# Loading the first four pairs' expert weights inside the recurrence instead of among the sorted rows

## The chip, the cores and the metric

The kernel runs on one core of one Trainium2 chip. The metric is the device time of one execution in microseconds, as the median of the runs shown. Without another unit, all times here are microseconds, and places in the trace are counted from the start of the profiled span.

## The reference, cut to what matters

Two layers are computed on 1024 tokens of 256 channels. Each layer normalises x, computes an attention part `s` and a mixture of experts `g` from the same normalised tokens, and adds `s * silu(g)` to x. The change lies in the second layer. Its attention part is a gated linear recurrence over the tokens with an output product and a small MLP behind it:

```python
def step(S, inp):
    qt, kt, vt, gt = inp
    S = S * jnp.exp(gt)[..., None] + kt[..., None] * vt[..., None, :]
    ot = jnp.einsum('bhk,bhkd->bhd', qt, S)
    return (S, ot)
...
logits = flat @ router_w
_, topk_idx = jax.lax.top_k(logits + router_bias, K)     # K = 4 of E = 64 experts
...
g = jax.nn.silu(jnp.einsum('nd,edf->nef', flat, wg))     # F = 64 hidden channels an expert
u = jnp.einsum('nd,edf->nef', flat, wu)
routed = jnp.einsum('ne,nef,efd->nd', comb, g * u, wd)
```

`wg` and `wu` hold 256 x 64 numbers for each expert, `wd` 64 x 256, all float32.

## The kernel before, in words

The second layer is `gated_linear_attention`. It is a row of blocks; all engines meet at the end of each. Two of them are touched.

**The recurrence's block.** It projects the tokens, routes them, and runs the recurrence in 16 steps (`STEPS = 2 * GK`), each with a scan on DVE over all tokens (L2159). PE sums a step's heads (`gathered_step`, L1941) and counts `o_step` up. Until step 7 PE also computes the output gates (`gates`) from the weights `wg`. Meanwhile POOL scatters each token's row to its four places in a DRAM tensor, `sorted_tokens`, in the order of the experts (L1807). A token has four experts, so there are 4096 sorted rows. The router also makes a table of windows: 64 main windows, one for each expert, of 128 sorted rows, and 32 extra ones for experts with more rows. SP writes the table to DRAM and reads it back (`store_table`, `table_loaded`). Last in SP's program come the loads of the first eight blocks of 256 sorted rows, `load_rows` (L1798), when all rows are scattered; there are eight row buffers.

**The pairs' block.** First comes the row stage. PE transposes the recurrence's output (`turn_state`, L2391, eight tiles) and the sixteen blocks of sorted rows (`turn_rows`, L2401); ACT copies the even blocks from PSUM to `xTs` (L2319), DVE the odd ones (L2214). When all are there, the 48 pairs of windows follow (`Blocks1`). They are worked in the order main, main, extra. For each pair q:

- SP loads its gate and up weights into one of four raw buffers and its down weights into one of eight down buffers (`Blocks1.load`, L1599 to L1609): three DMAs of 128 KB for a main pair; for an extra pair two reads of the table into registers and six DMAs of 64 KB. From q = 4 on it waits until pair q-4 is laid out, from q = 8 on until the down product of pair q-8 is done.
- POOL lays the weights out (`lay`, L1618), four pairs ahead at most.
- PE multiplies gate and up (`gate_up`, L1639, eight matmuls), two pairs ahead of down; ACT applies silu, DVE multiplies (`hidden`, L1693), PE multiplies down (L1651), ACT copies the result and stores it to DRAM.

Beside the pairs run the parts of the shared experts, of the output product and of the normalisation, each tied to a number of a pair (`side`). A pair with an even number from 0 to 14 carries one half of the shared experts' gate and up (L1494 to L1496, twelve matmuls).

The order of SP's queue in the pairs' block is written out by hand: row blocks 8 to 15, each when the block eight before it is turned, and behind every second of them the weights of one pair, so of the pairs 0 to 3; then the pairs from 4 on.

SBUF places are given by hand too. `shelf(start, end)` hands out places between two offsets in KB. The masks of the recurrence (`spread`, `gather_h`) lie at 165 to 171, the first products' weights (`wq`, `wk`, `wv`, `wg` and others) at 171 to 182, the router's work buffers at 182 to 194. The pairs' buffers lie from 165 on, over all of these, and so can be filled only when the recurrence has ended.

Of the kernel before, what the change touches and what calls it, by code (L numbers as in the profile page):

```python
# [13 lines left out]
P = 128  # L14
T = 1024
NT = T // P
D = 256
DC = D // P
# [22 lines left out]
E1, F1, K1 = 64, 64, 4  # L41
# [11 lines left out]
class Chain:  # L53
# [3 lines left out]
    def __init__(self, engine, done):  # L57
        self.engine, self.done, self.count = engine, done, 0
# [1483 lines left out]
class Blocks1:  # L1542
# [4 lines left out]
    PAIRS = WINDOWS // 2  # L1547
    EXTRA = OVER // 2
    RAW, LAID, DOWN, HIDDEN, GROUP = 4, 4, 8, 3, 4

    def __init__(self, nc, env, w, router, xTs, weights, results):
        self.psum, self.table, self.xTs = env["psum"], router.table, xTs
        self.gu_src, self.dn_src = [w["L1_ffn_" + k] for k in ("wg", "wu")], w["L1_ffn_wd"]
        self.y_dram = nc.dram_tensor("block_outputs", [WINDOWS * P, D], F32, kind="Internal").ap()
        sem = env["sem"]

        self.nc, self.at = nc, {}
        self.order = [pair for i in range(self.EXTRA) for pair in (self.EXTRA + 2 * i, self.EXTRA + 2 * i + 1, i)]
        self.raw_loaded = [sem(f"e1_ld{b}") for b in range(self.RAW)]
        self.dn_loaded = [sem(f"e1_dl{b}") for b in range(self.DOWN)]  # L1560
        self.main_stored = [sem(f"e1_ms{b}") for b in range(2)]
        self.extra_stored = [sem(f"e1_xs{b}") for b in range(2)]
        self.laid, self.gu_ready, self.silu_ready, self.h_ready, self.y_ready, self.y_done = (
            sem("e1_" + s) for s in ("la", "gu", "si", "h", "y", "yd"))
        self.raw = [weights(f"e1_raw{b}", [P, 2, 2, DC, F1]) for b in range(self.RAW)]
        self.gu = [weights(f"e1_gu{b}", [P, 2, DC, 2, F1]) for b in range(self.LAID)]
        self.dn = [weights(f"e1_dn{b}", [P, D]) for b in range(self.DOWN)]
        self.sg, self.hf = ([weights(f"e1_{n}{b}", [P, cols]) for b in range(self.HIDDEN)] for n, cols in (("sg", 2 * P), ("hf", P)))
        self.main_y = [results(f"e1_ym{b}", [P, 4, D]) for b in range(2)]
        self.extra_y = [results(f"e1_yx{b}", [P, 2, D]) for b in range(2)]  # L1570
# [127 lines left out]
def gated_linear_attention(nc, env, w, out):  # L1698
# [8 lines left out]
    def at(kb, name, shape, dt=F32):  # L1707

        return nc.alloc_sbuf_tensor_at("g_" + name, shape, dt, offset=int(kb * 1024))

    def shelf(start, end):

        place = [int(start * 1024)]

        def put(name, shape, dt=F32):
            here, size = place[0], int(np.prod(shape[1:])) * SIZE[dt]
            place[0] = here + -(-size // 32) * 32
            assert place[0] <= end * 1024, (name, place[0])
            return nc.alloc_sbuf_tensor_at("g_" + name, shape, dt, offset=here)
        return put  # L1720

    keep = shelf(194, 208)
    router = Router1(nc, env, w, keep)
# [27 lines left out]
    xTs = at(25, "xTs", [P, DC, SLOTS1 + P])  # L1751
    ROW_BUFFERS = 8
# [1 line left out]
    ogT, equal, wo = at(66, "ogT", [P, DC, T]), at(74, "equal", [P, NT, E1]), at(76, "wo", [P, DC, D])  # L1754
    shared.work_buffers(shelf(141, 157), shelf(58, 66))
    x2r, x2T_h, x2T_l = at(97, "x2r", [P, NT, D]), at(81, "x2T_h", [P, DC, T], F16), at(85, "x2T_l", [P, DC, T], F16)
    blocks = Blocks1(nc, env, w, router, xTs, shelf(165, 194), shelf(208, 224))
    mlp = at(58, "mlp", [P, 2, SplitWeights.SHARED - SplitWeights.W1], F16)
    yg = at(25, "yg", [P, NT, K1, D])
    late_at = shelf(141, 175)  # L1760
# [8 lines left out]
    def square(act, source, which, n):  # L1769
# [18 lines left out]
    v_spread, kv_ready, st_ready, qs_ready, o_step, oT_done, z_read, e_made, ln_made, dec_made = (  # L1788
        sem("g2_" + s) for s in ("v", "kv", "st", "qs", "o", "oT", "zr", "ea", "ln", "dc"))
    xs = nc.dram_tensor("sorted_tokens", [SLOTS1, D], F32, kind="Internal").ap()  # L1790
    STEPS = 2 * GK
    LATE_HALF = 3
    ROW_BLOCKS = SLOTS1 // (2 * P)
    rows_loaded = [sem(f"g4_rl{b}") for b in range(ROW_BUFFERS)]

    def load_rows(sp, i):
        b = i % ROW_BUFFERS
        sp.dma_start(rows[b][:, :, :], xs[2 * P * i:2 * P * (i + 1), :].rearrange("(t p) d -> p t d", p=P))\  # L1798
          .then_inc(rows_loaded[b], 16)
# [13 lines left out]
    with nc.Block() as block:  # L1813
        @block.sync
        def _(sp):
            split_stored(sp)
            for i, name in enumerate(("L1_attn_ln1_w", "L1_attn_ln2_w")):
                sp.dma_start(ln[:, i, :], w[name].rearrange("(c p) -> p c", p=P), allow_slow_non_contiguous=True).then_inc(ln_loaded[i], 16)
            for i, (dst, src) in enumerate(loads):
                sp.dma_start(dst[:, :, :], src.rearrange("(c p) n -> p c n", p=P)).then_inc(w_loaded[i], 16)  # L1820
            router.load(sp)
            sp.dma_start(wg2[:, :], w["L1_attn_Wkg2"]).then_inc(w_loaded[5], 16)
            sp.dma_start(bg2[:, :], w["L1_attn_bkg2"].rearrange("(p a) -> p a", a=1)).then_inc(w_loaded[6], 16)
            sp.dma_start(bg[:, :], w["L1_attn_bg"].rearrange("(a n) -> a n", a=1)).then_inc(w_loaded[7], 16)
            sp.wait_ge(y_ready, NT)
            shared.load(sp)
            router.store_table(sp)
            sp.wait_ge(xs_stored, 16 * NT * K1)
            sp.wait_ge(g_ready, NT // 2)
            for i in range(ROW_BUFFERS):  # L1830
                load_rows(sp, i)

        @block.gpsimd
        def _(pool):
# [345 lines left out]
    PAIRS, SHARED_HALVES = blocks.PAIRS, 2 * shared.QUARTERS  # L2180
# [25 lines left out]
    with nc.Block() as block:  # L2206
# [78 lines left out]
        @block.sync  # L2285
        def _(sp):
            sp.wait_ge(router.table_loaded, 16)
            for i in range(ROW_BUFFERS, ROW_BLOCKS):
                sp.wait_ge(rows_turned, i - ROW_BUFFERS + 1)
                load_rows(sp, i)  # L2290
                if i % 2:
                    blocks.load(sp, (i - ROW_BUFFERS) // 2)
            for q in range((ROW_BLOCKS - ROW_BUFFERS) // 2, PAIRS):
                blocks.load(sp, q)
                if q == WO_AT:
                    sp.dma_start(wo[:, :, :], w["L1_attn_Wo"].rearrange("(c p) n -> p c n", p=P)).then_inc(wo_loaded, 16)
# [322 lines left out]
def program(nc, w, out):  # L2619
    with ExitStack() as ctx:  # L2620
# [23 lines left out]
        with ExitStack() as layer0:  # L2644
            def tmp(name, shape, dt):
                return layer0.enter_context(nc.sbuf_tensor(name, shape, dt))
            env["gate0"] = tmp("gate0", [P, NT, D], F32)
            env["xT_h"], env["xT_l"] = tmp("xT_h", [P, DC, T], F16), tmp("xT_l", [P, DC, T], F16)
            env["head_weights"] = HeadWeights(nc, env, w, tmp)
            with ExitStack() as norm:  # L2650
                env["xn"] = norm.enter_context(nc.sbuf_tensor("xn0", [P, NT, D], F32))
                env["xnT"] = xnT = norm.enter_context(nc.sbuf_tensor("xnT0", [P, DC, T], F32))
                before = len(in_use)
                mixture0(nc, env, w)
                nc.clear_and_free_semaphores(in_use[before:])
                del in_use[before:]
                nc.all_engine_barrier()  # L2657
            env["split_rest"] = nc.dram_tensor("split_rest", [P, 2, SplitWeights.REST], F16, kind="Internal").ap()
            env["oT_h"], env["oT_l"] = tmp("oT_h", [P, H, T], F16), tmp("oT_l", [P, H, T], F16)

            env["qk"], env["sq"] = tmp("qk", [P, NT, 2, HD], F32), tmp("sq", [P, NT, 2, HD], F32)
            env["wo_halves"] = [env[k][:, :, :, :].rearrange("p n j d -> p (n j d)").bitcast(F16).rearrange("p (h e) -> p h e", e=D)
                                for k in ("sq", "qk")]
            attention0(nc, env, w)
            env["first_layer"] = list(in_use)
            gated_linear_attention(nc, env, w, out)
# [23 lines left out]
```

## Time and profile before

| | us |
|---|---|
| median of 3 runs | 1079.27 (1079.18 to 1079.59) |
| the profiled execution | 1080.21 |
| its span | 1078.4 |
| busy in the span: PE / DVE / ACT / POOL | 947.4 / 806.0 / 630.9 / 484.2 |
| mean granted clock of PE | 0.943 |

In the span, the recurrence ends at about 849.9, the row stage lasts from 851.9 to 871.1, and the pairs end at about 1016.

How the lines below are read. A line of the windows view gives a stretch, its length, then for PE, PEld, DVE, ACT and POOL the busy time with the number of instructions in brackets, the granted clock of PE as a share of 2.4 GHz, the busy share of the 16 DMA engines, and GB/s. A line of a timeline gives the start, the time taken, the engine, the line of the kernel, the operation, out<-in, the shape, and the number of instructions merged; in square brackets stands how long the engine was idle before it and what ended that. A line for one source line gives the duration of one as least/median/most in ns. A line of the waits gives who waited at which line for whom, the sum, the times, and the longest. "SPq" is SP's queue of DMA issues.

### The profile page before, as it was taken

To read this page: it belongs to the slowest core of one execution; us is meant where nothing else is said; L and a number is where in the kernel's file an instruction comes from. 1 tells how busy PE (TensorE), PEld (TensorE's weight loads), DVE (VectorE), ACT (ScalarE), POOL (GpSimd) and SP (SyncE) were. 2 spreads that over 40 slices of the span, in tenths; PEclk is the share of its full clock that TensorE was granted. 3 is DMA by queue.
4 is the path that set the end of the run, shared out by engine and by line. 5 is a ranking of instruction groups with operands and counts; after the bars stand their busy time and mean duration, and the time that the engine had idled before them with its cause. 6 is when DMAs were issued, how large, how long until landed. Compare 5 with 4: busy or idle time off the path is not lost. (4 is left out here: it accounts for less than half of the span.)

```text
span 1078.4 us, 18348 instructions
## 1 busy us (share of the span) xinstructions
PE 947.4 (88%) x6414; PEld 592.2 (55%) x6414; DVE 806.0 (75%) x1445; ACT 630.9 (58%) x1097; POOL 484.2 (45%) x385
## 2 busy tenths in 40 slices
PE   5976977999999999999999997899697789799797
PEld 4455754565555565555555552596243456577444
DVE  3958438999999999999999998255899537364267
ACT  3646037887888887888887887235210337446341
POOL 3130645556665556665556450200681027432273
PEclk9985988999999999999999999899899889799899
DMA  5475115788989889889879879501122266578632
GB/s 173 106 194 168 29 45 100 158 150 165 179 170 172 157 155 169 177 167 165 165 153 176 158 137 234 111 1 60 58 79 97 87 193 202 164 228 280 207 98 84
DMA packets 380881, 155.61 MB, mean 144 GB/s; under 512 B 287556, under 2 KB 378230, under 8 KB 380534
## 3 DMA queue, kind: packets, MB, share of 16 engines
q1 hardware_dynamic: 363286, 131.23, 56.1%
q10 hardware_dynamic: 14432, 14.81, 4.1%
q0 software_dynamic: 3072, 8.39, 2.3%
q8 instruction: 52, 0.85, 0.3%
q14 instruction: 39, 0.32, 0.1%
HBM read 60.93 MB, written 23.72 MB: 78 GB/s over the span
## 5 line engine op out<-in xcount | busy, mean ns | idle before, releaser
L940 DVE SCALAR_TENSOR_TENSOR a_halves<-a_ex,a_share,a_halves 128x1024 f16<-128x1024 f32 x128 | 190.5, 1488 | 36.9 <-ACT a_halves L934 34.9
L1237 DVE TENSOR_REDUCE a_nmax<-psum 128x1 f32<-128x1024 f32 x128 | 156.5, 1223 | 6.6 <-PE psum L1106 6.3
L1026 POOL TENSOR_TENSOR a_rnorm<-a_ss,a_power 128x8 f32<-128x8 f32 x32 | 67.9, 2121 | 194.1 <-DVE a_ss L1213 194.0
L934 ACT ACTIVATE a_halves<-a_ex,a_share 128x1024 f16<-128x1024 f32 x128 | 146.8, 1147 | 12.8 <-DVE a_share L1243 7.2
L1180 ACT ACTIVATE a_ex<-psum,a_nmax 128x1024 f32<-128x1024 f32 x128 | 142.6, 1114 | 0.5 <-DVE a_nmax L1237 0.5
L1088 PE MATMUL psum<-a_wh,xT_h 128*128 128x128 f16 (+1 forms) x512 | 115.8, 248 | 4.3 <-PEq L2657 2.0
L1089 PE MATMUL psum<-a_wl,xT_h 128*128 128x128 f16 (+1 forms) x512 | 115.6, 248 | 0.0
L1090 PE MATMUL psum<-a_wh,xT_l 128*128 128x128 f16 (+1 forms) x512 | 115.6, 248 | 0.0
L1118 PE MATMUL psum<-a_pT,a_vh 128*128 128x512 f16 x256 | 98.7, 385 | 10.5 <-DMA a_pT<-a_halves 10.5
L1120 PE MATMUL psum<-a_pT,a_vl 128*128 128x512 f16 x256 | 98.5, 385 | 0.0
L1119 PE MATMUL psum<-a_pT,a_vh 128*128 128x512 f16 x256 | 98.4, 384 | 0.0
L1102 PE MATMUL psum<-a_qkTh 128*128 128x512 f16 x256 | 76.7, 381 | 2.8 <-ACT a_ex L1180 2.8
L1693 DVE TENSOR_TENSOR g_e_hf<-psum,g_e_sg 64x128 f32<-64x128 f32 x96 | 28.2, 294 | 64.9 <-ACT g_e_sg L1659 58.4
L1104 PE MATMUL psum<-a_qkTl,a_qkTh 128*128 128x512 f16 x256 | 76.6, 381 | 0.0
L1106 PE MATMUL psum<-a_qkTh,a_qkTl 128*128 128x512 f16 x256 | 76.6, 381 | 0.0
L1618 POOL COPY g_e_gu<-g_e_raw 128x256 f32<-128x256 f32 x96 | 38.9, 438 | 78.0 <-DMA g_e_raw<-in_L_ffn_wu 62.6
L1807 POOL DMA_INDIRECT sorted_tokens<-g_xn,g_r_slot x32 | 42.5, 1328 | 69.6 <-DVE g_r_slot L1394 60.1
L1075 PE MATMUL psum<-ident,qk 128*128 128x128 f32 x256 | 40.9, 286 | 31.6 <-POOL qk L1029 28.5
L1159 ACT ACTIVATE sq<-psum 128x512 f32<-128x512 f32 x64 | 38.2, 597 | 45.3 <-PE psum L1090 45.3
L1166 ACT ACTIVATE a_qkTh<-psum,a_qk_scale 128x512 f16<-128x512 f32 x64 | 43.9, 687 | 33.3 <-PE psum L1075 29.1
L1029 POOL TENSOR_TENSOR qk<-qk,a_rnorm 128x1024 f32<-128x1024 f32 x32 | 61.5, 1921 | 2.5
L1639 PE MATMUL psum<-g_xTs,g_e_gu 128*128 x384 | 56.8, 297 | 5.2 <-POOL g_e_gu L1618 5.2
(389 smaller groups left out, 2409.2 us busy)
## 6 DMA issues: line engine op xcount, KB each, us to landing
block_outputs<-g_e_ym ACTq DMA_DIRECT2D x16, 512.0 KB, 3.6
split_rest<-a_e_wh SPq DMA_DIRECT2D x15, 384.0 KB, 3.2
wf<-in_L_ffn_W_gate SPq DMA_DIRECT2D x32, 128.0 KB, 2.6
wf<-in_L_ffn_W_up SPq DMA_DIRECT2D x32, 128.0 KB, 2.6
wf<-in_L_ffn_W_down SPq DMA_DIRECT2D x32, 128.0 KB, 3.0
g_rows<-sorted_tokens SPq DMA_DIRECT2D x16, 256.0 KB, 4.3
g_e_raw<-in_L_ffn_wg SPq DMA_DIRECT2D x32, 128.0 KB, 3.1
g_e_raw<-in_L_ffn_wu SPq DMA_DIRECT2D x32, 128.0 KB, 3.4
```

What stands on the lines that cost most here:

```text
L934: act.activation(halves[i % PB][:, :, 0, :], ex[m % 2][:, :].rearrange("p (k q) -> p k q", q=P), ACT.Copy, scale=share[:, m:m + 1]).then_i ...
L940: dve.scalar_tensor_tensor(halves[i % PB][:, :, 1, :], ex[m % 2][:, :].rearrange("p (k q) -> p k q", q=P), share[:, m:m + 1], halves[i % P ...
L1088: pe.matmul(dst, xh, wh, start=(c == 0), stop=False)
L1089: pe.matmul(dst, xh, wl, start=False, stop=False)
L1090: last = pe.matmul(dst, xl, wh, start=False, stop=(c == DC - 1))
L1102: pe.matmul(psum[:, bank + f, :], qh, kh[f], start=True, stop=False)
L1104: pe.matmul(psum[:, bank + f, :], qh, kl[f], start=False, stop=False)
L1118: pe.matmul(out, vh[:, k, :], ph, start=(k == 0), stop=False)
L1119: pe.matmul(out, vh[:, k, :], pl, start=False, stop=False)
L1120: last = pe.matmul(out, vl[:, k, :], ph, start=False, stop=(k == KT - 1))
L1180: act.activation(ex[m % 2][:, :], score_banks(m), ACT.Exp, bias=nmax[:, m % 2:m % 2 + 1], accum_out=total[:, m:m + 1]).then_inc(exp_ready, 1)
L1237: dve.tensor_reduce(nmax[:, k:k + 1], score_banks(m), AX.X, ALU.max, negate=True).then_inc(max_ready, 1)
```

## The change

The raw buffers, the laid-out buffers and seven of the eight down buffers move to 171 to 194, where the first products' weights and the router's work buffers lie, and the rest of the pairs' buffers to 165 to 171. Inside the recurrence's block, SP issues the loads of the pairs 0 to 3 behind the first eight row blocks. Ahead of them it waits until half of the recurrence's steps are summed (`o_step`, 8 of 16), by when the weights are read for the last time, and until the table is there. In the pairs' block SP then issues row blocks 8 to 15 with nothing between them, and the pairs from 4 on behind them.

```diff
-    def __init__(self, nc, env, w, router, xTs, weights, results):
+    def __init__(self, nc, env, w, router, xTs, early, weights, results):
...
-        self.raw = [weights(f"e1_raw{b}", [P, 2, 2, DC, F1]) for b in range(self.RAW)]
-        self.gu = [weights(f"e1_gu{b}", [P, 2, DC, 2, F1]) for b in range(self.LAID)]
-        self.dn = [weights(f"e1_dn{b}", [P, D]) for b in range(self.DOWN)]
+        self.raw = [early(f"e1_raw{b}", [P, 2, 2, DC, F1]) for b in range(self.RAW)]
+        self.gu = [early(f"e1_gu{b}", [P, 2, DC, 2, F1]) for b in range(self.LAID)]
+        self.dn = [(early if b < self.DOWN - 1 else weights)(f"e1_dn{b}", [P, D]) for b in range(self.DOWN)]
...
-    blocks = Blocks1(nc, env, w, router, xTs, shelf(165, 194), shelf(208, 224))
+    blocks = Blocks1(nc, env, w, router, xTs, shelf(171, 194), shelf(165, 171), shelf(208, 224))
...
             for i in range(ROW_BUFFERS):
                 load_rows(sp, i)
+            sp.wait_ge(o_step, STEPS // 2)
+            sp.wait_ge(router.table_loaded, 16)
+            for q in range(blocks.RAW):
+                blocks.load(sp, q)
...
             for i in range(ROW_BUFFERS, ROW_BLOCKS):
                 sp.wait_ge(rows_turned, i - ROW_BUFFERS + 1)
                 load_rows(sp, i)
-                if i % 2:
-                    blocks.load(sp, (i - ROW_BUFFERS) // 2)
-            for q in range((ROW_BLOCKS - ROW_BUFFERS) // 2, PAIRS):
+            for q in range(blocks.RAW, PAIRS):
                 blocks.load(sp, q)
```

## Rows read from the trace of the kernel before

**Rows 1.** Windows view, the row stage.
```profile
851.90:871.10 19.20, 14.01 (x81) 11.71 (x81) 5.53 (x8) 9.40 (x16) 3.22 (x9) 0.80 0.72 211
```

**Rows 2.** Windows view, stretches of two microseconds in and behind the row stage.
```profile
858.00:860.00 2.00, 2.00 (x15) 1.69 (x14) 0.69 (x1) 1.52 (x4) 0.74 (x2) 1.00 0.81 244
...
864.00:866.00 2.00, 0.86 (x6) 0.62 (x6) 0.69 (x1) 1.19 (x2) 0.14 (x1) 1.00 0.33 92
866.00:868.00 2.00, 0.21 (x1) 0.22 (x2) 0.00 (x0) 0.00 (x0) 0.61 (x2) 0.67 0.79 262
...
874.00:876.00 2.00, 2.00 (x11) 2.00 (x11) 1.90 (x4) 0.38 (x1) 0.77 (x3) 0.50 0.53 159
876.00:878.00 2.00, 2.00 (x11) 1.09 (x11) 1.89 (x5) 0.93 (x2) 0.74 (x2) 0.77 0.87 251
```

**Rows 3.** Timeline of PE, row blocks 8 to 15 and the first pairs.
```profile
858.94 1.39 PE L2401 MATMUL psum<-ident,g_rows 128*128 128x128 f32 x8
...
863.23 1.41 PE L2401 MATMUL psum<-ident,g_rows 128*128 128x128 f32 x8 [1.09 <-DMA g_rows<-sorted_tokens]
...
867.79 2.25 PE L2401 MATMUL psum<-ident,g_rows 128*128 128x128 f32 x8 [2.92 <-DMA g_rows<-sorted_tokens]
871.07 5.49 PE L1639 MATMUL psum<-g_xTs,g_e_gu 128*128 x24 [1.03 <-POOL g_e_gu L1618]
...
877.32 0.39 PE L1494 MATMUL psum<-g_xT_h,g_s_w 128*128 128x512 f16 x1
...
879.92 1.05 PE L1639 MATMUL psum<-g_xTs,g_e_gu 128*128 x8
880.91 0.70 PE L1651 MATMUL psum<-g_e_dn,g_e_hf 64*128 64x256 f32 x4
881.54 1.16 PE L1639 MATMUL psum<-g_xTs,g_e_gu 128*128 x8
```

**Rows 4.** Timeline of DVE, the copies of blocks 9, 11 and 15, a hidden product.
```profile
860.37 0.69 DVE L2214 COPY g_xTs<-psum 128x512 f32<-128x512 f32 x1 [0.90 <-PE psum L2401]
861.96 0.69 DVE L2214 COPY g_xTs<-psum 128x512 f32<-128x512 f32 x1 [0.90 <-PE psum L2401]
...
870.08 0.69 DVE L2214 COPY g_xTs<-psum 128x512 f32<-128x512 f32 x1 [4.70 <-PE psum L2401]
...
881.42 0.60 DVE L1693 TENSOR_TENSOR g_e_hf<-psum,g_e_sg 64x128 f32<-64x128 f32 x2 [1.64 <-ACT g_e_sg L1659]
```

**Rows 5.** Timeline of SP's queue, row blocks 12 to 15 around the third pair.
```profile
859.24 0.94 SPq L1798 DMA_DIRECT2D g_rows<-sorted_tokens  x2
861.24 0.38 SPq L1607 DMA_DIRECT2D g_e_raw<-in_L_ffn_wg  x1
...
865.03 1.10 SPq L1798 DMA_DIRECT2D g_rows<-sorted_tokens  x2
```

**Rows 6.** Source line view of the row loads, 850 to 870.
```profile
L1798 SPq DMA_DIRECT2D g_rows<-sorted_tokens x8: 360/450/1852, 852.9 to 865.7; - x8
...
DMA to landing us min/median/max: 2.7/3.6/4.6
```

**Rows 7.** Timeline of SP's queue inside the recurrence.
```profile
815.33 3.99 SPq L1798 DMA_DIRECT2D g_rows<-sorted_tokens  x8
```

**Rows 8.** Timeline of ACT, the copy that the eighth step releases.
```profile
814.67 1.02 ACT L2069 ACTIVATE g_oT<-psum 128x1024 f32<-128x1024 f32 x1 [1.12 <-PE psum L1941]
```

**Rows 9.** Windows view, the recurrence behind the first row loads.
```profile
824.00:850.00 26.00, 16.92 (x34) 5.45 (x32) 21.76 (x14) 0.13 (x1) 0.00 (x0) 0.80 0.00 0
```

**Rows 10.** Source line view of the recurrence's scans on DVE.
```profile
L2159 DVE TENSOR_TENSOR_SCAN g_state<-g_dec,g_kv x16: 2290/2291/2302, 765.9 to 842.5; 128x1024 f32<-128x1024 f32 x16
```

**Rows 11.** Waits, 886 to 1016, around the layout of weights.
```profile
POOL g_e_gu L1618 <- DMA g_e_raw<-in_L_ffn_wu: 45.7, 21, 4.7
...
PE psum L1639 <- POOL g_e_gu L1618: 4.1, 2, 2.2
```

**Rows 12.** Waits of SP's queue, 870 to 1012, its longest.
```profile
SPq L1595 <- PE psum L1651: 14.5, 7, 4.4
```

## The prediction, made before the changed kernel ran

> **What bounds the kernel now.** I read the windows by stage first, then the same stretch in windows of two microseconds, then the timelines of PE, SP and DVE in it, and last the waits of the stages behind it. The stretch that the change touches is the one between the recurrence and the pairs, 851.9 to 871.1: 19.2 us, in which PE is busy 14.0, DVE 5.5 and ACT 9.4 [rows 1], so no engine fills it. Sixteen blocks of sorted rows are turned there. Until block 11 they run at one pace: the copies of blocks 9 and 11 on DVE start 1.59 apart [rows 4]. Then PE waits twice for rows to land, 1.09 ahead of block 12 and 2.92 ahead of block 14 (one merged line each; block 15 has its own wait inside the second, whose eight transposes take 2.25) [rows 3]. Both are waits for SP's order of issue and not for the transfer: SP issues blocks 12 and 13 at 859.24, then goes through the third pair, whose two experts are read from the table, and comes to blocks 14 and 15 only at 865.03 [rows 5]. Block 14 needs only that block 6 is turned, which was so before the transposes of blocks 8 and 9 at 858.94 [rows 3]. So the bound is a queue: weights of pairs stand in front of rows that are wanted first.
>
> A second cost hangs on it. PE's granted clock is 1.00 (2.4 GHz) at 858 to 860, and after these waits it is 0.67 and then 0.50 (1.2 GHz) until it comes back between 876 and 878 [rows 2]. The first three pairs' gate and up products fall into that: 24 matmuls from 871.07 on take 5.49, where a pair's eight take 0.99 later (879.92 to 880.91) [rows 3].
>
> **The change part by part.** *Removed from the row stage:* 15 issues of weights on SP (three main pairs of three DMAs, one extra pair of six and two reads of the table). Behind it SP carries only the eight row loads, each released by the block eight earlier. Block 15's load is then issued as soon as block 7 is turned, near 859, instead of 865.6. A row load takes up to 4.6 to land [rows 6], so it is there by 863.6 to 864.1. PE comes to it when the steady pace brings it: DVE's copy of block 11 started at 861.96, of block 13 it is then 863.55, of block 15 865.14, so the transposes of block 15 run near 864.4. The copy of block 15 started at 870.08 [rows 4]. First term: 870.08 - 865.14 = 4.94. Were the landing 1 to 2 later than 4.6, PE would wait about 1 to 1.5 of it; that is the lower bound of this term, 3.5. It can't be much above 4.94, since the pace of 1.59 is a chain of transposes, copy and semaphore that nothing here shortens.
>
> *What is late next:* the copy of block 15, then the first gate and up. It started 0.99 behind that copy [rows 3, 4] and I keep this, so it starts at 866.13. The idle stretch of PE ahead of it is 1.2 at most, no longer than the 1.09 ahead of block 12, behind which the clock stayed up, 1.00 at 864 to 866 [rows 2, 3]; so I take the clock as 2.4 GHz there. From the first gate and up to the fourth it was 871.07 to 879.92, 8.85. At the full clock it is three times 0.99, one down product of 0.63 (880.91 to 881.54), and the shared product between, 877.32 to 879.92, 2.60, which ran at full clock already [rows 3]: 6.20. Second term: 2.65. No new wait stands in it: a pair's hidden product on DVE ends 2.10 behind the start of its gate and up (879.92 to 881.42 + 0.60) [rows 3, 4], and down comes 2.97 behind it. The second term is between 0 (the clock stays low) and 2.65.
>
> The page on the clock in the Trainium skill ("TensorE: Matmul & The Clock Gate", section "Part 4: PE-mode transpose") says that the full clock doesn't engage for transposes, since they don't count as a busy PE in the same way. By it the second term would be 0 and the sum 4.94. The trace disagrees: at 858 to 860 PE has nothing but transposes of rows and of states, and the granted clock is 1.00 [rows 2].
>
> *Added inside the recurrence:* the 15 issues, behind the first eight row loads on SP. SP issues those from 815.33 in 3.99 [rows 7]; then comes the new wait for the eighth step. ACT evacuates the eighth step's sum at 814.67 [rows 8], so the wait is over before SP gets there, and behind it on SP stand only these loads and the end of the block. They take about 9 (nine to fifteen issues near 0.5, and a table read of about 1.06 as at 860.18 to 861.24 [rows 5]), to 828 or so, 22 ahead of the block's end. The DMA engines move nothing from 824 to 850 [rows 9], so 1.57 MB (four pairs of 384 KB) lands for nothing. What it could cost is the recurrence, which DVE carries: its 16 scans last 2290 to 2302 ns, with rows landing at a full DMA beside some of them [rows 10], so I take 0 and bound it at 0.1.
>
> *Moved:* the raw, laid and most down buffers go to where the first products' weights lay, other small ones to the masks' place. The same instructions work on them with the same shapes; I take 0. POOL's copies of the first four pairs' weights now run at the start of the row stage, beside DVE's copies of rows. They ran beside them before too, later in the stage, and those copies of rows took 0.69 each [rows 4]; 0.
>
> *Does it last to the end?* From 871 to 1016 the loads are not far ahead: POOL waits 45.7 for raw weights from 886 on, and PE 4.1 in the end for POOL [rows 11]. A stretch bound by loads could start when it always did. But SP in turn waits 14.5, in seven waits, for down products [rows 12], that is for PE: the down buffers bound its lead to eight pairs. The loads' run therefore begins from a moment that PE sets, and shifts with PE. I carry the whole gain through. Behind the pairs nothing has a time of its own.
>
> Sum: 4.94 + 2.65 = 7.6. The profiled execution took 1080.21 with a span of 1078.4; it would be 1072.6 with a span of 1070.8. The median shown is 1079.27, 0.94 less, so 1071.7.
>
> **The rivals.** *The clock stays low* into the first pairs, whatever the rows do: 4.94 alone, 1074.3. For it: 1.2 GHz until 876, after a stretch in which PE was busy by fits; against it: the 1.00 at 858 to 860, and that the waits which went before the fall are the ones that go.
>
> *The gain is given back at the end*, because the weights and not PE set when the last pairs come: 1079.3. For it: POOL's 45.7 of waits for raw weights; against it: SP's seven waits for PE.
>
> *More than that*: four pairs of lead survive to the end and PE's 4.1 of waiting for POOL goes too [rows 11]: 11.7, 1067.6. Against it: a lead of four pairs is used up by the same eight-pair bound.
>
> *SP holds the recurrence's block open*, the rival on the slower side. All engines meet at the end of that block, and SP now has 15 more issues ahead of it. One row issue of the trace took 1.85, in the stretch with the weights and rows together, beside a median of 0.45 [rows 6]. SP has from 819.3 to about 849.9, 30.5, less 2 for table reads: at 1.9 for each issue it ends with the block, at 2.4 the whole gain is gone, and at 2.7 the block ends 12 late, 1083.7. For it: it starts right behind eight row loads; against it: those eight together took 3.99, and the DMA engines are empty from 824.
>
> **How the numbers follow.** Forecast 0.62; the clock stays low 0.14; more than that 0.09; given back 0.11; SP holds the block 0.04. About 0.2% (2.2 us) is what a measurement of this kernel can tell from no change. Faster by more: 0.62 + 0.14 + 0.09 = 0.85; within it 0.11; slower 0.04. The forecast's own range is 1070.2 (a little more clock) to 1073.2 (rows land up to 1.5 late). The range of 8 in 10 takes in the low clock and its late rows (1074.3 + 1.4, to 1076.0) and the edge of the larger gain: 1067.5 to 1076.0.
>
> **What would show it.** Right: SP's 15 issues lie between 819 and 830; the row stage's loads follow one another on SP; no PE wait for rows over 0.5; the last DVE copy of rows starts 13.3 behind the block's first transposes instead of 18.2; the first 24 gate and up matmuls take 3.0; the granted clock stays 1.00 from 858 on. The fourth gate and up starts near 872.3, and the last pair and the span's end are earlier by the same 7 to 8. Wrong: PE still waits for rows (the transfer was the bound, not the queue); 24 matmuls of 5.5 with a clock of 0.50; the fourth gate and up 7 earlier but the last pair not (given back in the loads); the block of the recurrence ends later than 849.9.

## The result, and the profile after it

The changed kernel takes 1072.97 us (median of 20 runs, 1066.27 to 1079.29), the kernel before beside it 1078.57 (20 runs, 1074.9 to 1082.45). The ratio is 0.995, interval 0.9933 to 0.9967: 5.6 us less, between 3.6 and 7.2. A second timing gave 0.9957 (0.9934 to 0.9981). The forecast was 7.6 less, to 1071.7. The profiled execution took 1076.02 with a span of 1074.3.

Windows of the changed kernel: the row stage, from the block's first transposes to the first gate and up; one stretch of two microseconds in it and two behind it; the recurrence beside the new loads, and behind them.

```profile
851.81:866.58 14.77, 12.98 (x80) 11.59 (x81) 5.53 (x8) 9.06 (x16) 3.07 (x9) 0.87 0.64 196
858.00:860.00 2.00, 1.85 (x14) 1.50 (x12) 1.02 (x2) 1.59 (x4) 0.00 (x0) 1.00 0.70 233
866.00:868.00 2.00, 1.42 (x12) 1.42 (x13) 0.28 (x1) 0.23 (x1) 0.12 (x1) 1.00 0.55 155
868.00:870.00 2.00, 1.60 (x14) 1.41 (x12) 1.77 (x3) 0.52 (x2) 1.36 (x4) 1.00 0.81 248
818.00:828.00 10.00, 6.26 (x18) 2.33 (x17) 9.86 (x7) 0.00 (x0) 0.00 (x0) 1.00 0.80 252
828.00:850.00 22.00, 15.29 (x27) 4.57 (x25) 17.63 (x12) 0.22 (x1) 0.00 (x0) 0.74 0.04 12
```

The row stage is 14.77 long instead of 19.20 [rows 1], with the same work in it on DVE (5.53) and nearly the same on ACT (9.06 and 9.40). The granted clock is 1.00 at 866 to 868, where it had been 0.67 [rows 2], and 1.00 in every two microseconds from there to 884.

PE's timeline of the changed kernel, block 15 and the first pairs:

```profile
864.02 0.64 PE L2403 MATMUL psum<-ident,g_rows 128*128 128x128 f32 x4
864.84 0.71 PE L2403 MATMUL psum<-ident,g_rows 128*128 128x128 f32 x4 [0.18 <-DVE g_xTs L2218]
866.58 2.05 PE L1639 MATMUL psum<-g_xTs,g_e_gu 128*128 x16 [1.03 <-issue]
869.02 1.15 PE L1639 MATMUL psum<-g_xTs,g_e_gu 128*128 x8 [0.40 <-DVE g_e_hf L1693]
870.11 0.70 PE L1651 MATMUL psum<-g_e_dn,g_e_hf 64*128 64x256 f32 x4
...
873.34 1.05 PE L1639 MATMUL psum<-g_xTs,g_e_gu 128*128 x8
```

Both waits for rows of [rows 3] are gone; what is left is 0.18 in front of block 15, for DVE to free a PSUM bank, as in front of the odd blocks before it. The 24 gate and up matmuls take 2.05 and 1.15 instead of 5.49, with a new wait of 0.40 between them, for the first pair's hidden product. DVE copies the turned rows at one pace to the end:

```profile
862.41 0.69 DVE L2218 COPY g_xTs<-psum 128x512 f32<-128x512 f32 x1 [0.90 <-PE psum L2403]
...
865.59 0.69 DVE L2218 COPY g_xTs<-psum 128x512 f32<-128x512 f32 x1 [0.90 <-PE psum L2403]
```

Blocks 11 and 15: 3.18 for two steps, 1.59 each, the pace of [rows 4], and 0.90 of idle where block 15's copy had 4.70.

SP's queue of the changed kernel: the row blocks inside the recurrence, the first and the last of the 15 loads of weights, the row blocks behind it, the next weights.

```profile
813.84 3.98 SPq L1798 DMA_DIRECT2D g_rows<-sorted_tokens  x8
817.92 0.83 SPq L1599 DMA_DIRECT2D g_e_raw<-in_L_ffn_wg  x1
...
827.23 0.47 SPq L1601 DMA_DIRECT2D g_e_dn<-in_L_ffn_wd  x1
853.41 6.17 SPq L1798 DMA_DIRECT2D g_rows<-sorted_tokens  x8
859.63 0.48 SPq L1599 DMA_DIRECT2D g_e_raw<-in_L_ffn_wg  x1
```

The 15 loads lie from 817.92 to 827.70, 22 ahead of the block's end, and block 15's load is issued by 859.6 instead of 865.6 [rows 5]. The rows land no faster than in [rows 6], and the recurrence's scans, with the weights landing beside some of them, are as long as in [rows 10]. First the time to landing of the row loads, then the scans:

```profile
DMA to landing us min/median/max: 2.8/3.9/4.6
```

```profile
L2163 DVE TENSOR_TENSOR_SCAN g_state<-g_dec,g_kv x16: 2290/2292/2298, 765.7 to 842.4; 128x1024 f32<-128x1024 f32 x16
```

The waits between 886 and 1005, and SP's own from 866 to 1000, answer to [rows 11, 12] and are still there:

```profile
POOL g_e_gu L1618 <- DMA g_e_raw<-in_L_ffn_wu: 49.8, 22, 6.0
...
PE psum L1639 <- POOL g_e_gu L1618: 5.9, 4, 2.5
```

```profile
SPq L1595 <- PE psum L1651: 12.3, 7, 2.3
```

Where the time went, in mean us of the traces there are by now (two executions of before, three of the changed kernel; the single values in brackets):

| stretch | before | changed |
|---|---|---|
| first transposes to first gate and up | 18.9 (19.17, 18.68) | 14.2 (14.77, 14.24, 13.55) |
| first to fourth gate and up | 8.3 (8.85, 7.75) | 6.76 (three times) |
| fourth to 18th | 43.1 | 43.1 |
| 18th to 22nd | 18.1 (20.07, 16.14) | 16.4 (16.21, 17.28, 15.78) |
| 22nd to last | 68.6 (67.7, 69.4) | 68.6 (69.2, 68.9, 67.6) |
| last to the MLP's first product | 7.5 (6.31, 8.66) | 7.9 (8.42, 7.91, 7.39) |
| MLP's first product to the end | 62.7 (61.3, 64.1) | 64.0 (64.0, 62.5, 65.4) |
| whole | 227.2 (226.5, 227.9) | 220.9 (222.5, 220.7, 219.5) |

The first two lines make 6.2 of the 6.3. The others differ as much between two executions of one kernel as between the kernels.

### The profile page after: what moved, and what is told of

Read it like the earlier page. It is cut to its first block and busy times, and to the rows that moved or that the text cites. A ratio compares the mean times of both kernels' runs of the same rounds, so it can differ in the third digit from the quotient of the medians.

```text
span 1074.3 us, 18349 instructions
## 1 busy us (share of the span) xinstructions
PE 945.2 (88%) x6414; PEld 589.3 (55%) x6414; DVE 806.0 (75%) x1445; ACT 630.6 (59%) x1097; POOL 483.1 (45%) x385
## 5 line engine op out<-in xcount | busy, mean ns | idle before, releaser
L1639 PE MATMUL psum<-g_xTs,g_e_gu 128*128 x384 | 54.2, 286 | 7.3 <-POOL g_e_gu L1618 5.9
```

## The experiments

Two parts of the change had to be told apart, the order of SP's queue and the early loading, and two terms, the rows' wait and the clock. A third part, the move of the buffers that early loading needs, was not run without early loading.

**The order alone.** The kernel before, with the weights behind all the row blocks and nothing loaded earlier or moved:

```diff
                 load_rows(sp, i)
-                if i % 2:
-                    blocks.load(sp, (i - ROW_BUFFERS) // 2)
-            for q in range((ROW_BLOCKS - ROW_BUFFERS) // 2, PAIRS):
+            for q in range(PAIRS):
                 blocks.load(sp, q)
```

> Only the order changes against the kernel before: SP issues row blocks 8 to 15 first and then pairs 0 to 47, all inside the pairs' block; no weights are loaded in the recurrence and no buffer moves. Theory A (the gain is SP's order: rows no longer stand behind weights): no PE wait for rows, the last DVE copy of rows 13.3 to 13.8 behind the first transposes (18.2 before), fourth gate and up near 873.5 to 874.5, total 4 to 6 us faster than before. Rival B (the gain is that 1.57 MB leaves the row stage, or the lead of four pairs): the first pairs wait for their weights, fourth gate and up behind 877, at most 2 us faster.

In the trace the rows' wait goes just as in the changed kernel: the last copy of rows starts 13.29 behind the first transposes, and the first 24 matmuls have the clock. What is late is the weights: POOL lays out the third pair's at 867.43, after 2.50 of waiting for them to land. DVE's last copy of rows and PE's timeline of this kernel:

```profile
864.63 0.69 DVE L2214 COPY g_xTs<-psum 128x512 f32<-128x512 f32 x1 [0.90 <-PE psum L2399]
```

```profile
865.62 2.05 PE L1639 MATMUL psum<-g_xTs,g_e_gu 128*128 x16 [1.03 <-POOL g_e_gu L1618]
868.31 1.15 PE L1639 MATMUL psum<-g_xTs,g_e_gu 128*128 x8 [0.65 <-POOL g_e_gu L1618]
...
882.43 0.70 PE L1651 MATMUL psum<-g_e_dn,g_e_hf 64*128 64x256 f32 x4 [0.99 <-DVE g_e_hf L1693]
```

The third gate and up waits 0.65 for POOL, and the down product at 882.43 waits 0.99 for a hidden product: from the first transposes to the 18th gate and up it is 65.7, against 64.6, 64.1 and 63.4 of the changed kernel's three traces and 71.1 and 69.5 of before's two. From the first transposes to the end it is 222.46. Yet twelve runs gave a median of 1080.14, ratio 1.0017 (0.9987 to 1.0047): no gain. Trace and times disagree, so it was run three times more, once beside the changed kernel:

> A second profile of the kernel that only changes SP's order (rows first, all weights in the pairs' block). Its twelve timed runs fall into two groups, four near 1073 and eight near 1081, and its first profile is of the lower one. If order alone is enough, the stretch from the first transposes to gate and up 17 repeats at about 65.7 us, as in its first profile, and the two groups come from behind it. If early loading matters, this stretch is several us longer in the other group, with PE waiting for weights in the first pairs.

> Order alone, timed beside the changed kernel. Its two profiles have the row stage and the first pairs within 0.8 us of the changed kernel's, so theory A expects it 4 to 6 us faster than before, at most 1.5 us behind the changed kernel. Its first twelve timed runs said no gain; if that repeats while the changed kernel gains, early loading does something that the profiles of order alone do not show, and that stays open.

> One more profile of order alone. Its 24 timed runs average no gain and spread over 15 us, while its three profiles have the stretch from the first transposes to the end as short as the changed kernel's. If this execution is one of those near 1080, the trace shows which stretch is longer: with weights late in the first pairs it is the one from the first to the eighteenth gate and up; if that stays near 65, the spread lies elsewhere and early loading is not what tells the two kernels apart. If it is again one near 1074, this stays open.

These traces too are as short as the changed kernel's: 220.99, 220.59 and 221.05 from the first transposes to the end (1075.03, 1072.89 and 1069.51 us). In all four the third gate and up waits for POOL (0.54 to 1.18), and the stretch to the 18th gate and up is 65.7, 64.9, 65.8 and 66.0: in the mean 1.5 longer than in the changed kernel and 4.7 shorter than before. The timed runs show no such gain: median 1078.17, ratio 0.9993 (0.9964 to 1.0021), where the changed kernel beside it had 1074.74.

The 26 executions of order alone average 1077.7, the 33 of the changed kernel 1073.8, though not all on one chip. The four of order alone with a trace average 1073.2, the other 22 1078.5; of the changed kernel the three with a trace average 1075.5, the other 30 1073.7. So the traces of order alone come from the short end of its spread (6 of the other 22 are as short), those of the changed kernel rather from the long end of its own, and trace beside trace flatters order alone. What a longer execution of order alone does differently, no trace shows. It isn't the clock over the whole span: the granted clock, which is on record for every execution, is 0.948 in the mean for both kernels.

So the traces show 1.5 that early loading adds, and the times ask for 3.4 (the medians beside each other) to 3.9 (all executions). Where the rest lies, in early loading or in the buffers' move that goes with it, isn't shown.

**Early loading, with weights again between the rows.** The changed kernel, with the pairs 4 to 7 where 0 to 3 had been:

```diff
                 load_rows(sp, i)
-            for q in range(blocks.RAW, PAIRS):
+                if i % 2:
+                    blocks.load(sp, blocks.RAW + (i - ROW_BUFFERS) // 2)
+            for q in range(2 * blocks.RAW, PAIRS):
                 blocks.load(sp, q)
```

> The changed kernel, but the loads of pairs 4 to 7 stand between row blocks 8 to 15, as those of pairs 0 to 3 did before; pairs 0 to 3 still come in the recurrence. Theory A: PE waits for rows again, last DVE copy of rows 17 to 18.5 behind the first transposes, the first 24 gate and up matmuls at 1.2 GHz again (about 5.4 us), total within 1.5 us of before. Rival B (early weights and their lead pay): first pairs start with full lead, 4 to 6 us faster than before.

PE's timeline and a window of this kernel:

```profile
860.46 1.41 PE L2405 MATMUL psum<-ident,g_rows 128*128 128x128 f32 x8 [2.87 <-DMA g_rows<-sorted_tokens]
...
864.43 1.98 PE L2405 MATMUL psum<-ident,g_rows 128*128 128x128 f32 x8 [2.34 <-DMA g_rows<-sorted_tokens]
867.44 5.25 PE L1639 MATMUL psum<-g_xTs,g_e_gu 128*128 x24 [1.03 <-issue]
```

```profile
868.00:870.00 2.00, 2.00 (x12) 2.00 (x11) 0.04 (x1) 0.38 (x1) 0.34 (x2) 0.50 0.00 0
```

Both waits are back, the last copy of rows is at 19.09, the clock is 0.50 behind it and the 24 matmuls take 5.25, though the first four pairs' weights have long been there. The time is 1080.28 (12 runs), ratio 1.0022 (1.0000 to 1.0044): the gain is gone. A lead in weights is no substitute for the order.

**The clock alone.** The kernel before, with transposes of the identity into an idle PSUM bank where PE would wait for rows; nothing of the computation is left out:

```diff
                 b = i % ROW_BUFFERS
+                for _ in range({12: 7, 14: 20, 15: 3}.get(i, 0)):
+                    pe.transpose(psum[:, 2, 0:P], ident[:, :], ident[:, :])
                 pe.wait_ge(rows_loaded[b], 16 * (i // ROW_BUFFERS + 1))
```

> The kernel before with 30 idle transposes of the identity into a PSUM bank that nothing reads, 7 ahead of row block 12, 20 ahead of block 14 and 3 ahead of block 15, where PE waits for rows; outputs unchanged. Theory A's second term (the waits let the clock fall and the first pairs pay): rows as late as before (last DVE copy about 18.2 behind the first transposes), granted clock 1.00 through the row stage, first to fourth gate and up 6.2 to 6.8 instead of 8.85, total 2 to 2.6 us faster. Rival C (transposes don't hold the clock, or the clock falls for another reason): 8.5 to 9, no change.

PE's timeline of this kernel, and the window in which PE has nothing but transposes:

```profile
867.11 2.35 PE L2397 MATMUL psum<-ident 128*128 128x128 f32 x20
...
871.95 2.05 PE L1639 MATMUL psum<-g_xTs,g_e_gu 128*128 x16 [1.04 <-issue]
874.40 1.15 PE L1639 MATMUL psum<-g_xTs,g_e_gu 128*128 x8 [0.40 <-DVE g_e_hf L1693]
...
878.72 1.05 PE L1639 MATMUL psum<-g_xTs,g_e_gu 128*128 x8
```

```profile
868.00:870.00 2.00, 2.00 (x19) 1.86 (x18) 0.00 (x0) 0.00 (x0) 0.09 (x1) 1.00 0.89 273
```

The rows come as late as before (last copy at 17.47), but the clock is 1.00 and the first to the fourth gate and up take 6.77, the changed kernel's 6.76. So the low clock here came from PE's waits, and this term is 2.1 by the profiled execution of before, 1.0 by the next one. From the first transposes to the end this trace takes 221.1, as short as the changed kernel's with the rows as late as before: such a length of one trace proves little. The time, 1078.22 (12 runs), ratio 0.9996 (0.9967 to 1.0025), can't tell a gain of that size from none.

**The same kernels again**, for what one execution leaves to chance, and the changed kernel timed a second time:

> A second profile of the changed kernel. Theory A: the row stage and the first to fourth gate and up repeat within 0.5 us (13.3 to 13.8 and 6.2 to 6.8), SP's early loads end before 830. Open is what follows: if the stretch from the fourth gate and up to the end differs from the first profile by several us while the row stage does not, the spread of the total lies in that stretch and not in the change.

> A second profile of the kernel before. Theory A: the row stage and the first to fourth gate and up repeat (18.2 and 8.85 within 0.7), since the waits for rows are SP's order. The stretch from gate and up 17 to 21 (20.07 in the first profile) and the stretch from 36 to the MLP's first product may differ by some us, as they do between the two profiles of the changed kernel (16.21 and 17.28).

> The changed kernel timed on the same chip and in the same rounds as the kernel that only changes SP's order. Theory A: about 5.6 us faster than before, as the two stretches from the first transposes to the end say (222.5 and 220.7 against 226.5 and 227.9).

The changed kernel's last copy of rows came at 13.24 and 12.56, before's at 17.68, and the first 24 matmuls of before took 4.59 this time:

```profile
868.73 4.59 PE L1639 MATMUL psum<-g_xTs,g_e_gu 128*128 x24 [1.03 <-POOL g_e_gu L1618]
...
876.48 1.05 PE L1639 MATMUL psum<-g_xTs,g_e_gu 128*128 x8
```

One execution gave 8.85 from the first to the fourth gate and up, the other 7.75. The waits for rows are there in both. The second timing is 1074.74 (12 runs) against 1078.96, the ratio 0.9957 given above, 4.2 less by the medians.

**What bounds the row stage now.** The changed kernel with four PSUM banks for the turned rows instead of two; with all 16 row blocks loaded inside the recurrence; and with both:

```diff
+    ROW_BANKS = (6, 7, 2, 3)
...
-                if i >= 2:
-                    pe.wait_ge(rows_dve if i % 2 else rows_act, i // 2)
+                if i >= 4:
+                    pe.wait_ge(rows_dve if i % 2 else rows_act, i // 2 - 1)
```

```diff
-    ROW_BUFFERS = 8
-    rows = [at(141 + 2 * b, f"rows{b}", [P, 2, D]) for b in range(ROW_BUFFERS)]
+    ROW_BUFFERS = 16
+    rows = [at((141 if b < 8 else 101) + 2 * b, f"rows{b}", [P, 2, D]) for b in range(ROW_BUFFERS)]
```

> The changed kernel with four PSUM banks for the transposed rows, row blocks 8 to 15 still loaded in the row stage. With both (four banks and all rows early) two blocks took 1.17 us instead of 1.59. Theory A: the rows' landing now stands in the way, since eight blocks of 256 KB released one by one can't follow at 0.59 us each: the copies keep 1.17 up to block 11 and then PE waits for rows, last DVE copy 11.5 to 13 behind the first transposes. If landing is no bound, 11.2 as with both.

> The changed kernel with all sixteen row blocks loaded in the recurrence and the two PSUM banks as they were. Theory A: the rows were in time already, so the row stage stays at 13.2 to 13.8, 1.59 for two blocks. If landing was a bound in the changed kernel it gets shorter.

> The changed kernel, with all sixteen row blocks loaded inside the recurrence (blocks 8 to 15 into places that are free until later: those of s1 and mix) and four PSUM banks instead of two for the transposed rows. What bounds the row stage now is the chain of transposes, copy and semaphore at 1.59 us for two blocks, not the rows: with four banks PE's own ten transposes (about 1.4 us) should set the pace. Theory A: row stage 1 to 1.5 us shorter than the changed kernel's 13.2 to 13.8, first to fourth gate and up unchanged, total 6 to 9 us faster than before. If the rows' landing were still a bound, loading them early would give more than 2 us; if neither, the row stage stays at 13.3.

DVE's copies of the last row blocks: four banks, all rows early, and both.

```profile
862.45 0.69 DVE L2220 COPY g_xTs<-psum 128x512 f32<-128x512 f32 x1 [0.56 <-PE psum L2405]
863.78 0.69 DVE L2220 COPY g_xTs<-psum 128x512 f32<-128x512 f32 x1 [0.64 <-PE psum L2405]
```

```profile
862.40 0.69 DVE L2218 COPY g_xTs<-psum 128x512 f32<-128x512 f32 x1 [0.90 <-PE psum L2403]
863.99 0.69 DVE L2218 COPY g_xTs<-psum 128x512 f32<-128x512 f32 x1 [0.90 <-PE psum L2403]
```

```profile
859.51 0.69 DVE L2220 COPY g_xTs<-psum 128x512 f32<-128x512 f32 x1 [0.48 <-PE psum L2405]
860.69 0.69 DVE L2220 COPY g_xTs<-psum 128x512 f32<-128x512 f32 x1 [0.48 <-PE psum L2405]
```

All rows early changes nothing: the pace is 1.59 and the last copy at 13.23, so the rows were in time already (1075.04 us, one run). Four banks bring the pace to 1.17, 1.25 and 1.33 in the end, the last copy to 11.39 (1067.92, one run); the trace lists no wait of PE for rows, and my expectation that their landing would now hold the last copy to 11.5 to 13 was wrong. Both together keep 1.18 to the end, 11.15, so late rows cost 0.24 at most. The time of both is 1071.87 (10 runs, 1064.52 to 1076.42), with before beside it at 1081.76 (14 runs): ratio 0.9909 (0.9878 to 0.9939), 9.9 less. That beats before by more than the change did; against the changed kernel itself it wasn't timed on one chip. Of the 6 to 9 by which its trace is shorter than the changed kernel's (213.3 against 219.5 to 222.5), the row stage accounts for about 2.

## Why the prediction was right, and by how much not

*The bound was SP's queue and not the transfer.* For the waits in the row stage this is shown from two sides: with the order mended, rows that take as long to land as before (up to 4.6) are waited for no more; with weights put back between the rows, the waits return although those weights are other ones, and the rows land no slower (median 3.6, against 3.9 in the changed kernel).

*First term, 4.94.* Measured 4.7 as a mean of the traces (18.9 to 14.2). The last copy of rows was to start 13.3 behind the first transposes; it did at 13.78, 13.24 and 12.56. The pace of 1.59 held, and nothing new was late in the stage. The three differ by where the first copy starts and by the first step (1.84, 2.13 and 1.59); in the kernel before it was 2.16, so the one pace that I gave it until block 11 holds from its third copy on only.

*Second term, 2.65: the term that was mis-sized.* It measured 1.5 (8.3 to 6.76). One reason, 0.56 of the 1.1 missing, lies on the side of the changed kernel: I took 6.20 as the length at full clock and wrote that no new wait stands in it. At that pace the third gate and up, which writes to the first pair's PSUM bank, comes before DVE has read that bank for the first pair's hidden product, and waits 0.40; what makes the other 0.16 isn't shown. I had looked at the hidden product's distance to down alone, and not to the gate and up behind it that needs its bank. The wait is there in the order alone (as 0.65, for POOL) and in the kernel with idle transposes (0.40). The other reason, 0.55, lies on the side of before: 8.85 was one execution's, and a second gave 7.75, with its first 24 matmuls at 4.59 instead of 5.49. A price read from a stretch at low clock is one draw out of several.

*The clock.* It stayed at 1.00 through the row stage's end and the first pairs, as forecast, and the rival with a low clock falls. PE's idle stretch ahead of the first gate and up was 1.03; I had allowed 1.2 and called it no longer than 1.09, which it wasn't by that sum. The kernel with idle transposes bears out the row on which this rested: PE doing nothing but transposes had 1.00 there too, against the rule quoted from the Trainium skill ("TensorE: Matmul & The Clock Gate", "Part 4: PE-mode transpose").

*Inside the recurrence, 0.* The scans are 2290 to 2298 with the DMA engines at 0.80 beside them, and SP is done at 827.7, so the rival in which SP holds the block open falls. (The full DMA that I wrote of beside the scans before was 0.88 at 816 to 820 and 0.78 at 820 to 824.) The row stage's own start can't show a cost below some microseconds: it lies between 846.8 and 854.4 in the traces of all these kernels, at 851.9 and 850.1 in the two of before.

*Carried to the end.* At the 18th gate and up the profiled execution was 6.5 ahead, counted from the first transposes, at the last pair 8.8, at the end 4.0. From the 22nd to the last gate and up both kernels take 68.6 in the mean, so the loads take nothing of the gain back; behind the pairs the lead moves by some us from execution to execution, and over the traces of both it is 6.3. The rival with more than that needed PE's waits for POOL to go, and they grew from 4.1 to 5.9.

*What stays open, and what was luck.* I had put the whole gain on the order. In the row stage the traces agree; the times don't: order alone has no gain that can be measured, 1078.2 beside the change's 1074.7. Early loading, or the move of the buffers with it, is worth something that the prediction put at nothing; the traces show 1.5 of it. So the time that came out right does not bear out the whole of the mechanism. Its closeness is luck in part too: 1071.7 is 1.3 off, while the difference of 7.6 is 2.0 off, because the kernel before measured 0.7 less this time.

## What to carry to other kernels

When an engine waits for a small transfer, look first at what stands ahead of it in the issuing queue: here weights that were needed later than the rows cost 4.7 us of the row stage, and the recurrence into which they were moved showed no cost: its scans stayed at 2292 ns, and the DMA engines' share behind the loads was 0.04. A wait of PE has a second price in the clock of what follows, which varies between executions, so take it from several. A bank that frees in time at the old pace has to be looked at again at the new one. And a few traces can all come from one end of a kernel's spread, so a gain that they show has to be timed as well.

## What I had not expected of the hardware

The same program, in the same place, has its clock back in one execution and not in the next. Windows of four microseconds between the 18th and the 22nd gate and up, first the profiled execution of before, from 4 behind the 18th on, then the second one from the same place on:

```profile
927.00:931.00 4.00, 2.56 (x16) 1.64 (x14) 1.48 (x4) 0.57 (x2) 3.23 (x6) 0.64 0.31 83
931.00:935.00 4.00, 2.66 (x12) 2.53 (x12) 0.00 (x0) 1.46 (x4) 1.16 (x1) 0.50 0.34 98
935.00:939.00 4.00, 2.71 (x9) 1.68 (x9) 1.97 (x4) 1.52 (x4) 0.74 (x2) 0.50 0.71 216
```

```profile
923.60:927.60 4.00, 3.51 (x16) 2.68 (x14) 1.01 (x3) 0.77 (x2) 3.24 (x6) 0.60 0.31 93
927.60:931.60 4.00, 2.17 (x16) 1.67 (x16) 1.25 (x5) 2.29 (x7) 1.89 (x3) 1.00 0.43 131
```

Both start at about 0.6. Then the first stays at 0.50 for eight microseconds, and the stretch took 20.07; the second is at 1.00 from 927.6 on, and it took 16.14. These 4 us are most of what the change is worth, and of the experiments some were near the one value (19.83, 20.07) and some near the other (15.75, 16.01). That is why the account above leans on stages and on many runs, and not on two spans.
